# Earlier loads for the third stage, h in the adjacency's place, and a second bank for the last tile

## The reference, cut to what matters

```python
fusion = x.reshape(b, n * d)                                   # b 2048, n 50, d 32, t 2
adj = jnp.einsum('bn,tnm->btm', fusion, masker_param) + masker_bias
adj = jax.nn.relu(adj).reshape(b, t, n, n)
adj = adj / (adj.sum(axis=-1, keepdims=True) + 1e-06)
m = jnp.einsum('btnd,de->btne', h, weight[0])                  # h starts as x
m = jnp.einsum('btnm,btmd->btnd', adj, m)
gates = m @ w_ih.T + b_ih + h @ w_hh.T + b_hh
r, z, ng = jnp.split(gates, 3, axis=-1)                        # sigmoid, sigmoid, tanh(r * ng)
h = (1.0 - z) * ng + z * h
xr = h.reshape(b, t * n * d)
xr = (xr - xr.mean(axis=0)) / jnp.sqrt(xr.var(axis=0) + 1e-05) * bn_gamma + bn_beta
h = xr.reshape(b, t, n, d)
h = (h - lmu) / jnp.sqrt(lvar + 1e-05) * ln_gamma + ln_beta    # over t, n and d
w = jax.nn.softmax(jnp.squeeze(h @ attn_w.T + attn_b, -1), axis=-1)
out = jnp.einsum('btn,btnd->btd', w, h)
```

## Time and profile before

| | |
|---|---|
| median of 3 runs | 2314.57 us (2312.24 to 2316.13) |
| the profiled execution | 2318.24 us |
| its span | 2316.5 us |
| PE busy | 2198.9 us (95%) |
| DVE busy | 1091.0 us (47%) |
| ACT busy | 962.2 us (42%) |
| POOL busy | 136.2 us (6%) |
| mean granted TensorE clock | 0.973 |

### The profile page before, as it was taken

The page is one execution under the profiler, slowest core; times in us unless marked ns, Lnnn a source line. Parts: engine busy times, 40 slices in busy tenths (PEclk is TensorE's granted clock), DMA queues, the critical chain, the costliest instruction groups (busy, mean ns, idle before and its releaser), DMA issues. The chain is left out here.

```text
span 2316.5 us, 34741 instructions
## 1 busy us (share of the span) xinstructions
PE 2198.9 (95%) x12302; PEld 1737.8 (75%) x12302; DVE 1091.0 (47%) x2177; ACT 962.2 (42%) x1637; POOL 136.2 (6%) x124
## 2 busy tenths in 40 slices
PE   8999999999999999999999999299999999975888
PEld 7888888888888888888888888277777777752333
DVE  4433233332345223333233332178888888873656
ACT  4322122221234212222122221088888988865551
POOL 0000000000000000000000000011101111104340
PEclk9999999999999999999999999699999999986899
DMA  6421222212234222221222211577777677619440
GB/s 208 151 75 44 88 91 90 74 45 88 92 128 143 64 90 90 91 69 50 89 90 91 72 48 27 124 171 184 186 201 181 188 199 181 181 65 261 122 119 5
DMA packets 341744, 264.06 MB, mean 114 GB/s; under 512 B 169334, under 2 KB 302998, under 8 KB 339990
## 3 DMA queue, kind: packets, MB, share of 16 engines
q1 hardware_dynamic: 323546, 225.69, 34.5%
q10 hardware_dynamic: 18144, 37.69, 5.0%
HBM read 195.65 MB, written 67.70 MB: 114 GB/s over the span
## 5 line engine op out<-in xcount | busy, mean ns | idle before, releaser
L340 PE MATMUL psum<-w_hi,x_lo 128*128 128x500 f32 x2080 | 823.0, 396 | 8.6 <-DVE w_lo L216 8.6
L340 PE MATMUL psum<-w_lo,x_hi 128*128 128x500 f32 (+1 forms) x2080 | 811.0, 390 | 0.0
L340 PE MATMUL psum<-w_hi,x_hi 128*128 128x500 f32 x1920 | 745.1, 388 | 0.0
L276 DVE TENSOR_REDUCE rows<-u 128x10 f32<-128x500 f32 x160 | 107.7, 673 | 893.5 <-ACT u L229 892.8
L340 PEld LDWEIGHTS psum<-w_hi,x_lo 128*128 128x128 f32 x2080 | 392.1, 188 | 84.4 <-issue 7.9
L340 PEld LDWEIGHTS psum<-w_lo,x_hi 128*128 128x128 f32 (+1 forms) x2080 | 392.5, 189 | 73.2
L340 PEld LDWEIGHTS psum<-w_hi,x_hi 128*128 128x128 f32 x1920 | 361.7, 188 | 72.9
L235 ACT COPY at<-psum 125x512 f32<-125x512 f32 x160 | 93.8, 586 | 677.4 <-PE psum L321 677.4
L229 ACT ACTIVATE u<-psum 128x500 f32<-128x500 f32 x160 | 94.1, 588 | 342.4 <-PE psum L340 342.3
L674 PE MATMUL psum<-adj_sb,xs_sb 100*64 100x100 f32 x2048 | 200.6, 350 | 30.1 <-DMA xs_sb<-xz 30.1
L674 PEld LDWEIGHTS psum<-adj_sb,xs_sb 100*64 100x64 f32 x2048 | 144.4, 149 | 73.9 <-issue 63.7
(11 more groups left out here) (160 smaller groups left out, 2284.8 us busy)
## 6 DMA issues: line engine op xcount, KB each, us to landing
w_raw<-W SPq DMA_DIRECT2D x140, 500.0 KB, 7.9
adjT<-at SPq DMA_DIRECT2D x160, 250.0 KB
adj_sb<-adjT SPq DMA_DIRECT2D x32, 1250.0 KB
xs_sb<-xz SPq DMA_DIRECT2D x16, 1600.0 KB
hF<-hC ACTq DMA_DIRECT2D x96, 256.0 KB, 6.7
h<-hF SPq DMA_DIRECT2D x64, 256.0 KB, 4.5
xg_sb<-xg ACTq DMA_DIRECT2D x14, 800.0 KB, 8.0
h<-hF SPq DMA_DIRECT2D x48, 192.0 KB, 3.7
```

The costliest lines, as they stand in the source:

```text
L276: nc.vector.tensor_reduce(rows[:, 0], u[:, c2], AX.X, ALU.add).then_inc(dve_step, 1)
L340: last = nc.tensor.matmul(mm_out(w % 2), a[0:r, k, cols], b[0:r, k, :], start=k == 0 and n == 0, stop=k == KF and n == 1)
```

## The change

Buffers that both stages use are now allocated once, outside of them, in a tuple `Shared`: the statistics, the identity, nine of the twelve small tensors, and an arena of 128 x 25600 numbers. In stage 3 the arena holds h of two blocks, ordered by sets. In stage 2 its first part holds the two slots of adjacency and x (10496 numbers each), its tail hC, r_gate and the weights' raw forms. Sets 0 to 4 of block 0 take 9728 numbers and so lie in slot 0 alone.

- SyncE issues nine of the twelve loads in stage 2 behind the loads of tiles 2 and 3, counted by early_loaded. Behind the loop it waits until tile 14 (the last in slot 0) is aggregated and until tiles 0 to 3 of hF are stored, then issues the 20 loads of sets 0 to 4 of block 0. The load of ident falls away.
- For tile 15, batches of odd number are turned into bank 0 instead of bank 7, and batch n waits for the copy of batch n - 2 alone.
- In stage 3 SyncE issues the 8 loads of sets 5 and 6, then spread and pool_mask, and as before block 1 behind spread_ready. VectorE waits for early_loaded where it waited for loaded, and for loaded ahead of the pool columns. ScalarE begins with a square root of one element behind the second setup step, takes the root of the variance without waiting for loads, and waits for loaded and casts spread between sets 1 and 2 of block 0's squares.

```diff
+SETS = [(n, list(range(n, FC, QC))) for n in range(QC)]
+SET_AT = [sum(len(cs) for _, cs in SETS[:n]) for n in range(QC)]
+EARLY_SETS = 5
+A_ADJ, A_XS = TN * SH, SH * 2 * D
+A_SLOT = A_ADJ + A_XS
+A_TAIL = 2 * A_SLOT
+def load_set(sp, shared, hF, i, n):
+    at = slice(SET_AT[n], SET_AT[n] + len(SETS[n][1]))
+    h = shared.arena[:].rearrange("p (i c b) -> p i c b", i=2, c=FC)
+    for k in range(CB):
+        sp.dma_start(h[:, i % 2, at, k * P:(k + 1) * P], hF[i * CB + k, :, slice(n, FC, QC), :]).then_inc(shared.h_loaded[i % 2][n], 16)
...
-        turn_bank = psum[:, 7 * BANK:8 * BANK]
+        def turn_bank(tile, n):
+            bank = 0 if isinstance(tile, int) and tile == TILES - 1 and n % 2 else 7
+            return psum[:, bank * BANK:(bank + 1) * BANK]
...
             iteration(0, True)
+            for dst, src in early_loads(shared, ins):
+                sp.dma_start(dst, src).then_inc(shared.early_loaded, 16)
             with sp.Fori(1, TILES // 2 - 1) as it:
                 iteration(it, True)
-            iteration(TILES // 2 - 1, False)
+            sp.wait_ge(ax_done, (TILES - 1) * ROUNDS)
+            for n in range(len(batches)):
+                sp.wait_ge(hC_stored[n], 16 * CB)
+            for n in range(EARLY_SETS):
+                load_set(sp, shared, hF, 0, n)
...
-                wait(pe, hC_ready, tile * len(batches) + n)
+                wait(pe, hC_ready, tile * len(batches) + (n - 1 if isinstance(tile, int) and tile == TILES - 1 and n else n))
...
+def early_loads(shared, ins):
+    return [(shared.quarter[:], ins["quarter"]), (shared.score_mask[:], ins["score_mask"]),
+            (shared.square_mask[:], ins["square_mask"]), (shared.fold_out[:], ins["fold_out"]), (shared.par[:], ins["par"]),
+            (shared.aw[:], ins["aw"]), (shared.ab[:], ins["attn_b"].partition_broadcast(P)),
+            (shared.rowpar[:], ins["rowpar"]), (shared.t_mask[:], ins["t_mask"])]
...
+        loads = [(spread_raw, ins["spread"]), (pool_mask[:], ins["pool_mask"])]
...
-            load_h(0)
+            load_h(0, EARLY_SETS)
+            for dst, src in loads:
+                sp.dma_start(dst, src).then_inc(loaded, 16)
             sp.wait_ge(spread_ready, 1)
             load_h(1)
...
-            dve.wait_ge(loaded, 16 * len(loads))
+            dve.wait_ge(shared.early_loaded, 16 * len(early_loads(shared, ins)))
...
             step(V.tensor_tensor(ALG[:], A[:], par[:, 2], ALU.mult))
+            dve.wait_ge(loaded, 16 * len(loads))
...
-            act.wait_ge(loaded, 16 * len(loads))
-            nc.scalar.copy(spread[:].rearrange("p c f -> p (c f)"), spread_raw).then_inc(spread_ready, 1)
+            act.wait_ge(step_done, 2)
+            nc.scalar.activation(warm[:], eps[:], ACT.Sqrt)
...
-            squares(0, *range(QC))
+            squares(0, 0, 1)
+            act.wait_ge(loaded, 16 * len(loads))
+            nc.scalar.copy(spread[:].rearrange("p c f -> p (c f)"), spread_raw).then_inc(spread_ready, 1)
+            squares(0, *range(2, QC))
```

More of the change, by code:

```diff
@@ L13 @@
 from concourse import mybir
+from collections import namedtuple
 from contextlib import ExitStack
@@ L384, in stage2, with in_tail @@
         sem = lambda name: ctx.enter_context(nc.semaphore(name))
-        adj = sb("adj_sb", [2 * N, 2, TN, SH])
-        xs = sb("xs_sb", [2 * N, 2, SH, 2 * D])
+        stats, ident = shared.stats, shared.ident
+        slots = shared.arena[0:2 * N, 0:A_TAIL].rearrange("p (r w) -> p r w", r=2)
+        adj = slots[:, :, 0:A_ADJ].rearrange("p r (t s) -> p r t s", t=TN)
+        xs = slots[:, :, A_ADJ:A_SLOT].rearrange("p r (s d) -> p r s d", s=SH)
+        tail = [A_TAIL]
+        def in_tail(rows, cols):
+            tail[0] += cols
+            return shared.arena[0:rows, tail[0] - cols:tail[0]]
+        hC = in_tail(P, FC * P).rearrange("p (c b) -> p c b", c=FC)
+        r_gate = in_tail(P, RC)
+        wd = in_tail(P, 4 * P).rearrange("p (a b c) -> p a b c", a=2, b=2)
+        wT4 = in_tail(D, P)
+        wih = in_tail(D, 3 * D)
+        whh4 = in_tail(P, 3 * D)
+        assert tail[0] <= 2 * FC * CW
         xg = sb("xg_sb", [P, 2, ROUNDS, N * QB])
@@ L498, in evacuate @@
                 nc.scalar.copy(hC[:, c0:c1, :].rearrange("p c b -> p (c b)"),
[L499 removed]
+                               turn_bank(tile, n)[:, 0:(c1 - c0) * P]).then_inc(hC_ready, 1)
             def store(tile, n):
@@ L799, in stage3 @@
         k_done, cols_ready = sem("k_done"), sem("cols_ready")
-        h_loaded = [[sem(f"h_loaded{p}{i}") for i in range(QC)] for p in range(2)]
+        h_loaded = shared.h_loaded
         sq_ready, sq_used, sums_done = sem("sq_ready"), sem("sq_used"), sem("sums_done")
@@ L828, in stage3, with load_h @@
         block = ctx.enter_context(nc.Block())
[L830 to L834, removed]
+        loads = [(spread_raw, ins["spread"]), (pool_mask[:], ins["pool_mask"])]
         @block.sync
         def _(sp):
[L838 to L844, removed]
+            def load_h(i, first=0):
+                for n in range(first, QC):
                     if i >= 2:
-                        sp.wait_ge(pr_ready, FC * (i - 2) + 1 + max(order.index(c) for c in range(n, FC, QC)))
-                    for k in range(CB):
-                        sp.dma_start(h[:, p, cs, k * P:(k + 1) * P], hF[i * CB + k, :, cs, :]).then_inc(h_loaded[p][n], 16)
+                        sp.wait_ge(pr_ready, FC * (i - 2) + 1 + max(order.index(c) for c in SETS[n][1]))
+                    load_set(sp, shared, hF, i, n)
             def store(sp, i):
@@ L1046, in square @@
                     wait(act, sq_used, g - SQ_BUFS + 1)
-                    nc.scalar.activation(sq[:, g % SQ_BUFS], h[:, i % 2, c, :], ACT.Square, bias=Csq[:, c:c + 1],
+                    nc.scalar.activation(sq[:, g % SQ_BUFS], h_of(i, c), ACT.Square, bias=Csq[:, c:c + 1],
                                          scale=A[:, c:c + 1]).then_inc(sq_ready, 1)
@@ L1051, in square @@
                     wait(act, sqp_used, g - SQ_BUFS + 1)
-                    nc.scalar.activation(sqp[:, g % SQ_BUFS], h[:, i % 2, c, :], ACT.Square, bias=Csq[:, c:c + 1],
+                    nc.scalar.activation(sqp[:, g % SQ_BUFS], h_of(i, c), ACT.Square, bias=Csq[:, c:c + 1],
                                          scale=A[:, c:c + 1]).then_inc(sqp_ready, 1)
@@ L1165, in sums_of @@
                     pe.wait_ge(h_loaded[i % 2][c % QC], 16 * CB * (i // 2 + 1))
-                    MM(q_bank[D * j:D * j + D, :], score_cols[:, c], h[:, i % 2, c, :], start=n == 0, stop=n == QC - 1 and 0 < j < 2)
+                    MM(q_bank[D * j:D * j + D, :], score_cols[:, c], h_of(i, c), start=n == 0, stop=n == QC - 1 and 0 < j < 2)
                 for k in batches[n]:
@@ L1280, in program @@
         stage1(nc, psum, ins["xT"], ins["W"], adjT, ins["ident"])
-        with nc.sbuf_tensor("stats", [P, TILES, FC, 6], fp32) as stats:
-            stage2(nc, psum, ins, adjT, hF, stats)
-            stage3(nc, psum, ins, hF, stats, out)
+        with ExitStack() as ctx:
+            sb = lambda name, shape: ctx.enter_context(nc.sbuf_tensor(name, shape, fp32))
+            sem = lambda name: ctx.enter_context(nc.semaphore(name))
+            shared = Shared(arena=sb("arena", [P, 2 * FC * CW]), stats=sb("stats", [P, TILES, FC, 6]), ident=sb("ident2_sb", [P, P]),
+                            quarter=sb("quarter_sb", [P, FQ, P]), score_mask=sb("score_mask_sb", [P, FC, D]),
+                            square_mask=sb("square_mask_sb", [P, D]), fold_out=sb("fold_out_sb", [P, T * D]),
+                            par=sb("par_sb", [P, 4, FC]), aw=sb("awF_sb", [P, 1]), ab=sb("abF_sb", [P, 1]),
+                            rowpar=sb("rowpar_sb", [TN, 3, D]), t_mask=sb("t_mask_sb", [TN, T]),
+                            early_loaded=sem("early_loaded"),
+                            h_loaded=[[sem(f"h_loaded{p}{i}") for i in range(QC)] for p in range(2)])
+            stage2(nc, psum, ins, adjT, hF, shared)
+            stage3(nc, psum, ins, hF, shared, out)
 def masks(np, dtype):
```

39 lines of the change are left out of this document (16 added, 23 removed).

## The result

The changed kernel takes 2344.53 us (median of four runs, 2337.41 to 2354.96) against 2314.68 us for the kernel before (2312.24 to 2316.13). The ratio is 1.0134, with a 95% interval of 1.0108 to 1.016: it is **slower by 1.3%**, 30 us, where 17 us less were forecast.

What follows compares the result with a forecast made beforehand. TensorE, busy 95% of the span, bounds the kernel; the change works in the hole between second and third stage. Savings of 3.8 + 15.3 - 1.7 = 17.4 us take the median from 2314.57 to 2297 us, range 2292 to 2304.

Steps and rivals of the forecast that it cites:

- loads in the second stage: Second stage: nine small loads and twenty of h delay nothing, 2 us spare; cost 0, bound 0 to 1.
- Rival 3: Second stage: nine early loads hold tile 4's adjacency and idle TensorE; 2325 us at 30 us late; chance 0.03.
- The second bank: Last tile's turning: batches start 1.15 us apart instead of 1.88, saving 3.8 us (2.8 to 4.5).
- Rival 2: Last tile's turning: ScalarE or VectorE holds batches at 1.85 us, 3.8 us lost, 2301 us; chance 0.08.
- The start of the third stage: First memset to Csq: waits for loads go, 10.23 us instead of 25.57, saving 15.3 us (14.8 to 15.5).
- Giving back: Third stage, ScalarE: 1.1 us wait for masks plus 2.86 cast minus 2.23 stall; 1.7 us lost (0.6 to 5.7).
- The stall of 2.23 us: Third stage: ScalarE's fifth square for TensorE waits 2.23 us for a free buffer; gone once the cast comes before.
- VectorE's wait for the pool mask: Third stage, ahead of the pool columns: uses 5.4 of 18.19 us idle before the first softmax step; costs nothing.
- Rival 4: Third stage: block 1's h loads become the bound at 171 GB/s, 2301 us; chance 0.07.
- The sum: Whole kernel: 3.8 + 15.3 - 1.7 = 17.4 us saved, median 2297 us.

Runs made afterwards that it cites:

- the aligned arena: The changed kernel with 384 bytes of unused SBUF ahead of the arena and 128 behind, so it starts at byte 16896: 2301.36 us, ratio 0.9943.

## Why the prediction was wrong

**The step that failed** is the one that costed loads in the second stage at nothing (0, with 0 to 1 as its bound); the stage came out 38.4 us longer. It looked at what the change adds to the queues, and not at what it does to the 48 loads that were there already: they write to another place. That the adjacency goes into the arena was read from the diff as a change of names. The slack it had worked out, 2 us in a tile's 35.1, was right, and was the whole cover. Stretches in which the adjacency is moved (all engines, clock, DMA share, GB/s), one of the kernel before and two of the kernel after:

```profile
1709.00:1725.00 16.00, 16.00 (x140) 12.44 (x139) 13.51 (x30) 13.62 (x27) 1.05 (x1) 1.00 0.91 197
```

```profile
1724.00:1740.00 16.00, 16.00 (x128) 12.76 (x129) 11.48 (x23) 12.70 (x25) 1.05 (x1) 0.92 0.87 159
1762.00:1778.00 16.00, 16.00 (x138) 12.71 (x135) 13.68 (x30) 13.65 (x26) 1.05 (x1) 1.00 0.94 172
```

At 197, 159 and 172 GB/s a tile's 2.56 MB take 13.0, 16.1 and 14.9 us: 1.9 to 3.1 us more for each tile, around the slack of 2. That fits a stage in which some tiles wait and others don't. And six of the seven stalls are followed by the half clock, so that waits of 17.8 us in all go with 13.3 us more of busy time.

The Trainium skill has this rule, in DMA: Bandwidth & Descriptors, section on how a descriptor splits into AXI transactions. By it a piece is cut into transactions of 256 bytes that start at multiples of 256, so that a piece that starts off such a multiple takes one more. By that rule a 256-byte piece goes from one transaction to two and a 512-byte piece from two to three. The page speaks of what is read; the runs show it for where a load writes. The size isn't the rule's: the issue time rises by 37% and not by 100%, and h gains 17% and not 50%. The beats of 32 bytes that the page counts as well would set 64 bytes off below 128 bytes off; here both cost the same by the time.

**Rival 3** named the symptom, the adjacency of later tiles late, TensorE idle and the clock down, and gave 2325 us for tile 4 being 30 us late; it came to 2344, spread over many tiles. Its cause was wrong: with the early loads still there and the arena aligned, nothing waits. It was given 0.03.

**The other steps**, read in the kernel after or on the aligned arena:
- The second bank: 3.8 forecast, 3.74 in the timeline, 4.2 between medians. Rival 2 is out. The Trainium skill, TensorE: Matmul & The Clock Gate, section on HAM oscillation, tells of no further gain from double-buffering PSUM in another kernel; in this one it gained. The stores are not evenly 1.15 apart but between 1.07 and 1.37.
- The start of the third stage: Csq at 10.23 forecast and 10.23 measured, and no DMA before LA.
- Giving back: ScalarE's wait for spread and the pool mask is the **mis-sized term**. It was put at 1.1 us and measured 2.38 on the aligned arena and 3.39 in the kernel after, inside its bounds of 0 and 5.1; traces with the same order of loads have 1.90 to 3.39. The stall of 2.23 us went as forecast. (The prediction counts six loads between spread and the last of the twelve; there are five, which changes nothing.)
- VectorE's wait for the pool mask (7.70 us in the kernel after) cost nothing, as forecast: 18.90 us of idle still stand before its first softmax step.
- Rival 4: no version that loads h early waits for block 1's h, and 48 GB/s more for h in the kernel before bring nothing. That speaks against it.

**The sum.** On the aligned arena the profiled execution took 2301.52 us, 16.7 less than the 2318.24 of the kernel before; 17.4 were forecast, 16.1 with the wait as measured. That these agree so well is partly luck. By the two traces 1.7 us of the 16.7 lie in the first stage and 0.2 in the second's rounds, where nothing was to be gained; the turning gave 3.8 and the third stage 11.2, from its first memset to the end (222.4 us instead of 233.6), where 15.3 - 1.7 = 13.6 were forecast. Of the 2.4 missing, 1.4 are in the giving back, which is 3.1 us at the first softmax step instead of 1.7; 1.0 lies behind that step and is not explained.

By medians the saving is 13.3 to 13.5. The forecast carried what it had worked out from the rows of one execution over to the median in full, and that execution stood 3.7 us above the median. Executions of the kernel before differ by 10 us (2308.56 to 2318.53), and the time goes with the mean granted clock: the three at 0.972 took 2317.1 us on average, the two at 0.978 2310.1. The traced one, at 0.973, was among the slow ones, and the 1.7 us of the first stage are part of its 3.7.

What isn't shown: the inside of the DMA engine. The runs show that the time depends on the start modulo 256 and on the length of the pieces. That it is an extra transaction for each piece is the page's account and fits them in kind, not in size. Nor is it shown why it is mostly every second tile that waits.

## What to carry to other kernels

When buffers are merged, moved or allocated in another order, work out where each of them starts in a partition, modulo 256 bytes, before and after, and look first at those that are filled in short pieces (256 or 512 bytes); a pad of some floats is the whole repair. A load "as before" is only as before if source, destination and piece length all are. And where a stream has 2 us of slack in 35, price every thing that touches its rate, for behind the slack stands not only the wait but, in most cases here, the half clock that follows it.

## What the runs showed of the hardware

- Loads in pieces of 256 bytes whose destination starts 64 or 128 bytes off a multiple of 256: the issue of a tile's adjacency takes 11.7 to 12.0 us at 128 off and 10.6 at 64 off instead of 8.75, that of x behind it 11.8 to 13.2 instead of 9.05, and the kernel 1.25 to 1.44% more. Between 64 and 128 the time makes no difference. A start at an odd multiple of 256 is as good as a multiple of 512.
- Pieces of 512 bytes, 64 bytes before or 128 behind a multiple of 256: 290 to 294 GB/s, against 335 to 346 at a multiple, in stretches with nothing but these loads at full flow. Pieces of 16384 bytes: no difference.
- A load that is queued behind others pays for them long after: nine small loads ahead of spread made the cast wait 6.98 us instead of 2.38, although their own users waited for nothing.
- A wait of TensorE of 1.79 to 4.42 us in the rounds was followed or accompanied by a granted clock of 0.50 for 3 to 6 us, six times of six; one of 0.79 us was not.
